# Squares for the first variance in a ViT block: made by VectorE behind the centring in place of ScalarE

## The reference

```python
h = _L0_tok_ref(x, W, b)                       # patches @ W.T + b + positional embedding
h = concatenate([cls_tok, h])                  # (64, 197, 256)
h = h + attn(_layernorm(h))                    # 16 heads, a cubic in place of exp, weights w_qkv, w_out
h = h + ffn(_layernorm(h))                     # 4 experts, 256 -> 1024 -> 256, gated by a sigmoid

def _layernorm(x, axis=-1, eps=1e-05):
    m = jnp.mean(x, axis=axis, keepdims=True)
    v = jnp.var(x, axis=axis, keepdims=True)
    return (x - m) / jnp.sqrt(v + eps)
```

## Time and profile before

| | |
|---|---|
| median of 3 runs | 3924.07 us |
| the profiled execution's own time | 3922.82 us |
| its span, first to last instruction | 3920.8 us |
| granted TensorE clock | 0.995 of full speed |
| TensorE matmul busy | 3865.7 us (99%) |
| TensorE weight load busy | 3396.0 us (87%) |
| VectorE busy | 2816.0 us (72%) |
| GpSimd busy | 2794.4 us (71%) |
| ScalarE busy | 2386.6 us (61%) |

### The profile page before, as it was taken

One profiled execution on the slowest core, in us unless ns is written; L12 is line 12 of the kernel. 1 busy time (PEld: TensorE's weight loads), 2 busy tenths in 40 slices (PEclk: granted clock), 3 DMA queues, 4 the chain that ended last, 5 costly groups with the idle time before them and its releaser, 6 DMA issues.

```text
span 3920.8 us, 86888 instructions
## 1 busy us (share of the span) xinstructions
PE 3865.7 (99%) x30148; PEld 3396.0 (87%) x30148; DVE 2816.0 (72%) x4316; ACT 2386.6 (61%) x4404; POOL 2794.4 (71%) x3527
## 2 busy tenths in 40 slices
PE   7899999999999999999999999999999999999998
PEld 4788888888888888888888888888888888888888
DVE  5777777777777777777777777777777777767763
ACT  5665566655566655666555666556665566655563
POOL 5666777767777667777677776677776777766775
PEclk8999999999999999999999999999999999999999
DMA  7344444444444444444444444445444444444455
GB/s 246 92 136 139 134 135 144 134 143 136 129 142 138 139 138 130 139 141 135 141 138 129 143 136 140 142 125 144 141 134 140 140 128 139 137 140 129 132 151 147
DMA packets 776545, 545.54 MB, mean 139 GB/s; under 512 B 157624, under 2 KB 701752, under 8 KB 775096
## 3 DMA queue, kind: packets, MB, share of 16 engines
q1 hardware_dynamic: 768096, 539.30, 47.0%
q10 hardware_dynamic: 8024, 0.70, 0.1%
HBM read 518.48 MB, written 21.30 MB: 138 GB/s over the span
## 4 chain that ended last, share of the span: by engine, by line
PE 95%; ACT 1%; POOL 1%; DVE 1%; issue 1%; DMA 0%; ACTq 0%; POOLq 0%; SPq 0%; DVEq 0%
PE ps L1362 67%; PE ps L1446 5%; PE ps L1461 5%; PE ps L1475 5%; PE ps L1560 4%; PE ps L1569 3%; PE ps L1577 2%; PE ps L1544 1%; PE ps L1538 1%; PE ps L1550 1%; PE ps L1526 1%; PE ps L1532 1%; ACT probs L731 0%; DVE lows L1071 0%; PE ps L1358 0%
## 5 line engine op out<-in xcount | busy, mean ns | idle before, releaser
L1362 PE MATMUL ps<-xn,w1s 128*128 128x197 f32 x4096 | 909.8, 343 | 3.4 <-ACT hT L692 2.3
L1362 PEld LDWEIGHTS ps<-xn,w1s 128*128 128x128 f32 x4096 | 676.6, 189 | 142.7 <-issue 132.4
L1362 PE MATMUL ps<-hT,w_s 128*128 128x197 f32 x4064 | 783.6, 330 | 3.9 <-issue 3.7
L996 DVE SCALAR_TENSOR_TENSOR probs<-probs,ps 99x788 f32<-99x788 f32 x512 | 483.4, 970 | 322.9 <-ACT probs L731 322.8
L1362 PEld LDWEIGHTS ps<-hT,w_s 128*128 128x128 f32 x4064 | 691.3, 190 | 5.9 <-issue 4.2
L583 POOL TENSOR_TENSOR hT<-hT 128x197 f32<-128x197 f32 x508 | 330.0, 650 | 513.8 <-ACT hT L707 509.0
L1362 PE MATMUL ps<-xt,w1s 128*128 128x197 f32 x3072 | 681.1, 330 | 3.3 <-ACT hT L698 1.7
L576 POOL TENSOR_SCALAR hT<-hT 128x394 f32<-128x394 f32 x496 | 626.2, 1263 | 13.9 <-DVE hT L1118 13.9
L1071 DVE TENSOR_REDUCE lows<-ps 99x8 f32<-99x1576 f32 (+1 forms) x256 | 460.3, 1799 | 219.2 <-PE ps L1461 219.2
L1362 PE MATMUL ps<-hT,w_a 128*128 128x197 f32 x3048 | 590.9, 329 | 0.2 <-DVE yw L1136 0.2
L1362 PEld LDWEIGHTS ps<-xt,w1s 128*128 128x128 f32 x3072 | 538.4, 190 | 36.3 <-DVE hT L1124 3.4
(11 more groups left out here) (143 smaller groups left out, 6204.1 us busy)
## 6 DMA issues: line engine op xcount, KB each, us to landing
w_s<-w_sums SPq DMA_DIRECT2D x508, 256.0 KB, 3.6
w_a<-in_w SPq DMA_DIRECT2D x384, 256.0 KB, 3.3
w1s<-w_sums SPq DMA_DIRECT2D x512, 192.0 KB, 2.6
w1s<-in_w SPq DMA_DIRECT2D x512, 128.0 KB, 2.3
x<-in_xT SPq DMA_DIRECT2D x30, 1188.0 KB, 7.4
w1s<-in_w SPq DMA_DIRECT2D x512, 64.0 KB, 1.9
w1s<-w_sums SPq DMA_DIRECT2D x512, 64.0 KB, 2.0
out_rows<-rows SPq DMA_DIRECT2D x244, 48.0 KB
```

Of the source, the lines that this page charges most:

```text
L996: nc.vector.scalar_tensor_tensor(out=part, in0=part, scalar=3.75, in1=ps[0:HB, 2 * half:2 * half + 2, 0:N], op0=ALU.add, op1=ALU.mult).the ...
L1362: return mm(place, weights, rows, start=start, stop=True, skip_group_check=True)
```

## The change

For the pairs from the third on (f = 2 to 31, so 30 pairs) ScalarE's square of `hc` goes, and VectorE multiplies `hc` by itself directly behind the instruction that makes it, with a wait for that instruction's own semaphore between. Input, output and semaphore of the squares stay the same; the first two pairs keep ScalarE's form.

```diff
@@ ScalarE, step
                     if has_b and k in (3, 4, 7):
                         log_of(b, k)
-                    if k == 1 and has_f:
-                        squares(f)
                     if k == 2 and has_f:
                         rs_of(f)
@@ VectorE
+            def squares_behind(f):
+                dve.wait_ge(hc_ready, at(f, 1, 1))
+                nc.vector.tensor_tensor(sums_of(f), hc[:], hc[:], ALU.mult).then_inc(sq_ready, 1)
@@ VectorE, step
                     if k == 1 and has_f:
                         centre(f)
+                        squares_behind(f)
                     if k == 1 and has_n:
                         sigmoid(n)
```

## The result

The changed kernel takes 3931.11 us (median of 17 runs, 3929.33 to 3932.75), the kernel before 3923.73 in the same sessions (17 runs). The ratio is 1.0018, with an interval of 1.0012 to 1.0025: 7.4 us more, +0.19%. The interval leaves out 1, so the loss is clear of the noise, and it is still within the 0.2% that the prediction took for the limit; the forecast was +5.5 us.

The account below looks back on a forecast made before the run. TensorE, its matmuls busy 99% of the span, was taken as the bound. Per step +0.46 - 0.25 = +0.21 us, over 29 steps 6.1, less 0.6 in step 1: 3924.07 + 5.5 = 3929.6 us, range 3926.5 to 3932.5.

Parts of the forecast that it names:

- Unit 2: TensorE's third weight load in unit 2 starts 0.52 us late behind VectorE's `up_sums_2`; TensorE loses 0.46 us a step.
- the first of the two prices: VectorE's added squares take 0.98 us each, with 1.54 us as the long price if GpSimd runs beside them.
- the slack: In unit 2 VectorE's `up_sums_2` may be 0.56 us late before TensorE loses time.
- The old wait of unit 4: TensorE's 0.25 us loss a step in unit 4, behind VectorE's `up_sums_2`, ends because TensorE arrives 0.46 us later.
- Rival (1): Unit 4 goes on losing 0.25 us as its VectorE chain moves along with TensorE; 3936.8 us, chance 0.16.
- Behind unit 4: After unit 4 the chain starts anew from TensorE's own matmuls; nothing else there moves against TensorE.
- The sum: Net +0.21 us per steady step over 29 steps, 6.1 us, less 0.6 in step 1: +5.5 us.
- ScalarE's relief: Removing 30 squares of 0.90 us gains ScalarE's chain 0.05 us a step, 0.10 at most; almost nothing freed.
- Step 1: The first step with the change gains 0.6 us from ScalarE's earlier chain, bounds -0.75 and +1.0.
- (2), the port: GpSimd meets VectorE's squares in SBUF, so they take 1.54 us, net 0.77 a step; 3945.8 us, chance 0.06.
- (3), no stall: No wait arises in unit 2, so only ScalarE's chain gain of 0.05 to 0.10 counts; 3921.5 us, chance 0.18.
- (4), faster by over 0.2%: Unit 4's 0.25 a step ends, 7.3 us, with -0.75 in step 1, and unit 2 stays free; chance 0.03.

Follow-up runs that it names:

- e2: Changed kernel, but VectorE squares only the first feature block of `hc` and ScalarE squares the second; 3919.35 us, ratio 0.9989.
- e5: Changed kernel with VectorE's `up_sums_2` of unit 3 moved ahead of `refine_2` and `normal_rows`; 3929.76 us, ratio 1.0017.
- e4: Kernel before, with VectorE's `up_sums_2` of unit 3 moved ahead of `refine_2` and `normal_rows`; 3920.97 us, ratio 0.9991.
- e6: Changed kernel without squares on ScalarE or VectorE from the third pair on; GpSimd squares the first block, the variance omits the second; 3920.53 us.
- e7: Kernel before, ScalarE still squaring, plus the same VectorE multiplication behind the centring into a tile nobody reads; 3931.09 us, ratio 1.0020.
- e8: Changed kernel with VectorE's squares moved from behind the centring to behind unit 2's `up_sums_2`, where GpSimd works; 3936.66 us, ratio 1.0032.
- e1: Changed kernel with a second, unread VectorE multiplication of the same size ahead of its own squares; 3977.91 us, ratio 1.0135.

## Why the prediction was right, point by point

**Unit 2, forecast 0.46 a step.** Right. The third load is 0.49 late (0.66 - 0.17), TensorE loses 0.43 (1.38 - 0.95). The squares take 0.98, the first of the two prices, with GpSimd idle beside them. The rest is L1120 itself, which took 0.50 for 0.52 and stood 1.01 behind, not 1.02. e2 tests the slack from its other side, at 0.57 us of work, and finds its edge where it was said to be.

**The old wait of unit 4, forecast paid back.** Right. The changed kernel has no idle there, and e5, which takes the cause of the wait away, gains nothing on it. Rival (1), 3936.8 us, is refuted.

**Behind unit 4, forecast nothing.** Wrong, and the only step that failed: "I see nothing else there that moves against TensorE". The first polynomial of block 4 moves against it: relative to TensorE's own matmuls it is fixed, and TensorE now comes 0.25 sooner to the load that needs it. The load starts 0.15 late and 0.09 is lost. The row for it was in the trace of before, VectorE's timeline behind unit 4:

```profile
1830.50 0.97 DVE L996 SCALAR_TENSOR_TENSOR probs<-probs,ps 99x788 f32<-99x788 f32 x1 [0.50 <-ACT probs L731]
```

It ended at 1831.47 and `wqk` started at 1831.66, 0.19 later. Of those 0.19, 0.12 are what the signal takes, so only 0.07 us of slack was left here, 0.10 in the mean of the 28 steps (0.22 less 0.12), under a gain of 0.25: 0.25 - 0.10 is the 0.15 by which the load came late. The prediction looked for waits, and one that is short of being a wait has no name in any view. e4 shows this loss without any of the change's work.

**The sum.** Per step +0.43 - 0.25 + 0.09 = +0.27, against +0.21 forecast; the trace has 120.28 - 120.01 = 0.27. Over 29 steps 7.8 us, with step 1 at -0.5, is +7.3. The medians differ by 7.4. That they meet within 0.1 is closer than the runs can tell: the interval of the ratio is 4.7 to 9.8 us, and the two ends of the kernel, which this sum leaves out, vary by more. The steps are the evidence, and there the miss is the 0.09 at `wqk`, less 0.03 in unit 2. The range 3926.5 to 3932.5 is also wider below than its own bounds make it: 29 x 0.05 and the step 1 bounds give 3928.0 to 3932.6.

**ScalarE's relief, forecast 0.05 to 0.10, counted as nothing.** Right in both: e6 measures 0.09, and e7 shows that it is worth nothing beside the added work.

**Step 1, forecast -0.6.** Right, -0.49. e7 leaves ScalarE's squares in and keeps 118.50, so the gain is the removal's.

**The other rivals.** (2), the port: the mechanism is real but lies elsewhere, and it has no fixed price such as the 1.54 that the prediction took. By e8 and e1 the squares would take 0.98 and, if a GpSimd instruction runs when they start, what is left of it less 0.14: 0 where they come first (0.97 in e1), 0.22 in e8. The 1.54 of L1050 fits this too: it starts at 1827.98, and the GpSimd instruction ahead of L583, L617, ends at 1828.68, so 0.98 + 0.70 - 0.14 = 1.54. (3), no stall: refuted by unit 2; the load is forgiven 0.06 us and no more. (4), faster by over 0.2%: refuted, yet e2, e4 and e6 show what it would have been worth, about 0.1%.

## What to carry to other kernels

Work on an idle engine isn't free when what is queued behind it feeds the bound engine. Its price is its duration less the slack of that one follower, and both can be read before the move: here 1.02 - 0.56, with the first 0.6 us free, so that half of the work could move at a gain (0.09 us a step) where all of it was a loss. Second, an ended wait can give back less than it cost (here 0.16 of 0.25): ask which load comes next and how long before it its input was ready, even where the profile shows no idle. A load 0.19 us behind its releaser was already as good as on the path.

## What the runs showed of the hardware

- A weight load may be some 0.06 us late before the matmuls lose anything: 1.79 late cost 1.73 (e1), 0.49 late cost 0.43, 0.15 late cost 0.09 (both in the changed kernel), and 0.08 late cost 0.02 (e2). The signal from VectorE's end to a load took 0.05 to 0.06 us at `up_sums_2` and 0.12 at `wqk` and the variance.
- After 1.77 us of idle TensorE's granted clock fell to 0.50 in 4 of 28 otherwise equal steps of e1 and cost 123.25 - 121.58 = 1.7 us each; after the 2.32 us of idle behind the last centring it fell in 5 of the 11 traces. What sets these apart stays open.
- Where a VectorE multiplication with both inputs in SBUF and a GpSimd `tensor_tensor` in SBUF meet, they take turns: the one that came first keeps its time, and the one that came second ends its own time after a point 0.14 to 0.15 us before the first's end. Both can look slowed because each is second once (e8: 1.20 for 0.98, 1.22 for 0.61).
- The third centring, ahead of any changed instruction, starts 133.7 to 138.4 us into the span, at a mean granted clock of 0.85 to 0.90 until then. Single spans can't be compared to better than that.
